# Attention stage of a graph network: two score banks and four turning banks instead of three and three, weighing two steps behind instead of three, a new order of VectorE's steps

## The reference, cut to what matters

```python
q = ((x @ Wq[l].T + bq[l]) * scaling).reshape(n, H, DH)
k = (x @ Wk[l].T).reshape(n, H, DH)
v = (x @ Wv[l].T).reshape(n, H, DH)
scores = jnp.einsum('ehd,ehd->eh', q[tgt], k[srcidx])
m = jax.ops.segment_max(scores, tgt, num_segments=n)
p = jnp.exp(scores - m[tgt])
s = jax.ops.segment_sum(p, tgt, num_segments=n)
w = p / (s[tgt] + 1e-16)
agg = jax.ops.segment_sum(w[:, :, None] * v[srcidx], tgt, num_segments=n)
attn = agg.reshape(n, D) @ Wo[l].T + bo[l]
x = _batchnorm(x + attn, g1[l], beta1[l])
ff = jax.nn.relu(x @ W1[l].T + b1[l]) @ W2[l].T + b2[l]
x = _batchnorm(x + ff, g2[l], beta2[l])
```

## Time and profile before

| | |
|---|---|
| median of the runs | 3730.28 us (3718.55 to 3731.51, 3 runs) |
| the profiled execution | 3731.51 us |
| its span, first to last instruction | 3729.7 us |
| mean granted TensorE clock | 0.932 of full speed |
| TensorE busy with matmuls | 3060.9 us, 82% |
| VectorE busy | 2398.0 us, 64% |
| GpSimd busy | 2258.4 us, 61% |
| ScalarE busy | 1894.0 us, 51% |
| first and last score matmul | 1198.9 us and 3536.5 us |

### The profile page before, as it was taken

One profiled execution on the slowest core, in us unless ns is written; L12 is line 12 of the kernel. 1 busy time (PEld: TensorE's weight loads), 2 busy tenths in 40 slices (PEclk: granted clock), 3 DMA queues, 4 the chain that ended last, 5 costly groups with the idle time before them and its releaser, 6 DMA issues. The chain is left out here.

```text
span 3729.7 us, 71602 instructions
## 1 busy us (share of the span) xinstructions
PE 3060.9 (82%) x24162; PEld 2383.1 (64%) x24162; DVE 2398.0 (64%) x6716; ACT 1894.0 (51%) x3792; POOL 2258.4 (61%) x1979
## 2 busy tenths in 40 slices
PE   1461995465798999999999988997999999999982
PEld 1220442232475787888888877775887788888871
DVE  7898452232212777888888865116887788888858
ACT  0120342122222777777777751225777777777712
POOL 2888888888000777767777750005776777777703
PEclk9995997777899999999999988998999999999995
DMA  9444643433314999999999960218998999999804
GB/s 365 59 83 91 139 106 55 89 69 55 107 45 89 152 165 159 161 159 160 161 164 166 165 113 34 54 45 153 163 164 160 162 158 165 160 163 164 151 19 115
DMA packets 1332714, 476.46 MB, mean 128 GB/s; under 512 B 1286534, under 2 KB 1312159, under 8 KB 1323558
## 3 DMA queue, kind: packets, MB, share of 16 engines
q1 hardware_dynamic: 1191472, 440.24, 61.2%
q0 software_dynamic: 133120, 0.80, 3.6%
q10 hardware_dynamic: 7788, 31.21, 2.5%
HBM read 138.70 MB, written 70.75 MB: 56 GB/s over the span
## 5 line engine op out<-in xcount | busy, mean ns | idle before, releaser
L1174 DVE CUSTOM_DVE_ANT_0 prob<-s_ps,mask 125x500 f32<-125x500 f32 x1600 | 1063.3, 673 | 334.2 <-PE s_ps L1021 245.2
L952 POOL TENSOR_TENSOR staged<-prob,staged 125x500 f16<-125x500 f32 x960 | 1065.6, 1116 | 169.8 <-ACT staged L946 108.3
L1111 ACT ACTIVATE prob<-prob,neg_max 125x1000 f32<-125x1000 f32 (+1 forms) x960 | 954.1, 994 | 151.3 <-DVE scrap L1180 150.3
L1021 PE MATMUL s_ps<-keys,queries 128*125 128x500 f16 x3200 | 946.7, 378 | 26.0 <-DMA queries<-q_feat 19.5
L372 POOL DMA_INDIRECT counts<-count,cell x320 | 758.9, 2371 | 167.4 <-issue 95.0
L1052 PEld LDWEIGHTS o_ps<-values,across 125*125 125x125 f16 x7680 | 591.1, 139 | 227.1 <-issue 78.5
L1052 PE MATMUL o_ps<-values,across 125*125 125x128 f16 x7680 | 608.5, 222 | 60.0 <-DMA across<-staged 59.1
L946 POOL CAST staged<-prob 125x500 f16<-125x500 f32 x640 | 385.6, 603 | 418.9 <-ACT prob L1111 277.2
L1187 DVE TENSOR_TENSOR p_lo<-t_ps,p_hi 125x500 f16<-125x500 f32 x640 | 431.8, 675 | 74.5 <-ACT p_hi L1121 73.6
L1121 ACT CAST p_hi<-t_ps 125x500 f16<-125x500 f32 x640 | 359.5, 562 | 113.6 <-PE t_ps L1032 113.3
L1032 PE MATMUL t_ps<-identity,prob 125*125 125x125 f32 x2560 | 406.5, 281 | 0.1
(11 more groups left out here) (139 smaller groups left out, 3731.4 us busy)
## 6 DMA issues: line engine op xcount, KB each, us to landing
mask<-bias_rows SPq DMA_DIRECT2D x200, 218.8 KB
counts<-xt ACTq DMA_DIRECT2D x8, 3054.0 KB, 38.2
parts<-counts SPq DMA_DIRECT2D x20, 1093.8 KB
bias_rows<-edge_bias SPq DMA_DIRECT2D x20, 1093.8 KB
queries<-q_feat SPq DMA_DIRECT2D x160, 125.0 KB, 3.8
pair_row<-pair_flat SPq DMA_DIRECT2D x40, 437.5 KB
across<-staged SPq DMA_TRANSPOSE x960, 3.3
counts<-count,cell POOLq DMA_INDIRECT x320, 4.2
```

The lines of the kernel that those rows point to most:

```text
L952: engine.tensor_tensor(here[0:P, BPC:2 * BPC, 0:P], prob[u % PROBS][:, k * KC:(k + 1) * KC].rearrange("p (s c) -> p s c", s=BPC), here[0:P ...
L1021: mm = pe.matmul(s_ps[n % SB][:, 0:KC], lhsT=queries[b][:, h, part, :], rhs=keys[:, h, c * KC:(c + 1) * KC], start=(part == 0), stop=(part ...
L1111: act.activation(here, here, ACT.Exp, bias=neg_max[u % 4][:, :], accum_out=sums[u // H % 2][:, u % H, piece:piece + 1]).then_inc(exped, 1)
L1174: dve.tensor_tensor_reduce(out=prob[u % PROBS][:, at], in0=s_ps[n % SB][:, 0:KC], in1=bias[b][:, at], scale=1.0, scalar=MASKED, op0=ALU.ad ...
```

## The change

Five things change. The score banks become two and the turning banks four. TensorE weighs two chunks behind instead of three; with LAG, ScalarE's read_high moves to k = 2 and VectorE's read_low to k = 3. In VectorE's program low_half(u, k) and read_low(u - 1) now stand ahead of add_bias(u + 2, k). The steps T and O stand at k = 1 and k = 3 of h = 1, 2 and 3, two in each, and bn_stats one head earlier. TensorE's wait for `wo_sb` moves from the first O step to ahead of the layer's first score.

```diff
-SB = 3
-TB = 3
-HEAD0 = 5
+SB = 2
+TB = 4
+HEAD0 = 4
...
-LAG = 3
+LAG = 2
...
-EXTRA = {(1, 2): ("T", 0), (2, 0): ("T", 1), (2, 2): ("O", 0), (3, 0): ("O", 1), (3, 2): ("O", 2), (4, 0): ("O", 3)}
+EXTRA = {(1, 1): ("T", 0), (1, 3): ("T", 1), (2, 1): ("O", 0), (2, 3): ("O", 1), (3, 1): ("O", 2), (3, 3): ("O", 3)}
...
                 def times_wo(t, o):
                     n, r = use("O", t, o)
                     user_done(pe, n - TB)
-                    if t == 0:
-                        pe.wait_ge(wo_loaded, 16 * (layer + 1))
                     pe.wait_ge(agg_turned, 2 * (T0 + t) + 2)
...
+                pe.wait_ge(wo_loaded, 16 * (layer + 1))
                 for u in range(2):
                     for c in range(NKC):
                         score(u, c)
...
                 for u in range(UNITS):
                     for k in range(NKC):
+                        if k in BY_PE:
+                            low_half(u, k)
+                        if k == LAG + 1 and u > 0:
+                            read_low(u - 1)
                         if u + 2 < UNITS:
                             add_bias(u + 2, k)
-                        if k in BY_PE:
-                            low_half(u, k)
-                        if k == min(LAG + 1, NKC - 1) and u > 0:
-                            read_low(u - 1)
                         stage_lows(u, k + NKC)
```

## The result

The changed kernel takes 3830.73 us (median of 4 runs, 3824.95 to 3835.14), the kernel before 3728.45 us beside it: a ratio of 1.0279, with an interval from 1.0254 to 1.0303. It is slower by about 102 us; the forecast was 3810, with a range to 3859. The profiled execution's span is 3822.8 us, 93 us over the one before. There attention of layer 0 began some 9.5 us earlier than in the execution before (SyncE's first load of queries at 1182.72 in place of 1192.26 us), which is the stage ahead of it, untouched by the change; so some 102 us belong to attention here too.

The account below looks back on a forecast made before the run. TensorE, busy 914.77 of 960 us, was taken as the bound before. A tile of 51.6 us, 1.4 over 50.14, gave 55 us over 38 tiles; with 22.6 for wo, 3731.5 + 78 = 3810, range 3762 to 3859.

Parts of the forecast that it names:

- the wait for wo: At each layer's first score: TensorE waits for SyncE's last load, 11.4 + 11.2 = 22.6 us, uncovered.
- The circle through two banks: In plain units: a closed chain through TensorE, ScalarE, VectorE and two score banks takes 5.87 us, against TensorE's own 5.41.
- The second circle: VectorE's chain through maximum, exponentials, halves and adds: 5.6 to 5.75 us, longer than 5.41 but shorter than 5.87.
- The other units: Head 1: 6.87 us, as normalising delays VectorE; heads 2 and 3: 7.33 each, with two O; head 0: 5.87.
- the transposes: Weighs stand one step nearer to their DMA transposes: 0.4 us a tile taken, bounds nothing and 1.3.
- bn_stats: On VectorE after maximum of h = 3: delays score 2 of h = 4 in every second tile, 0.3 us.
- What was removed: At the first O step: TensorE's wait for ScalarE's copy of T, all 0.8 us a tile counted as gone.
- the first rival: The rival "TensorE stays the bound": tile at its floor of 47.6 us, 3657 us in all; chance 0.07.
- TensorE stays the bound: Rival: circle shorter than 5.41 us, waits gone, tile 47.6 us, 3657 in all; decides from 0.46 us; chance 0.07.
- the circle bites only in part: Rival: the circle costs 0.1 us a plain unit, not 0.46, and the tile takes some 49.6; chance 0.05.
- The transposes bind: Rival: with the shorter lag, weighs wait 2.0 us a tile in place of 0.4, 3871 us; chance 0.08.
- The clock falls: Rival: TensorE's pauses put 3.4 us of every tile at the lower clock level, 3875 us; chance 0.04.

Follow-up runs that it names:

- a1: Changed kernel with TensorE's wait for wo back at the first O step of tile 0: 3812.02 us, ratio 1.0231 to the kernel before.
- b4: Kernel before with two score banks and four turning banks alone: 3740.36 us, ratio 1.0026.
- b5: Kernel before with VectorE's new order alone (low half and read_low ahead of the add): 3743.02 us, ratio 1.0025.
- b7: Kernel before with two score banks, four turning banks and VectorE's new order together: 3801.38 us, ratio 1.0199.
- a2: Changed kernel with three score banks and three turning banks again: 3782.47 us, ratio 1.0147 to the kernel before.
- a3: Changed kernel with VectorE's old order again (add_bias ahead of low_half and read_low): 3797.16 us, ratio 1.0180 to the kernel before.
- b3: Kernel before with a lag of two alone: 3764.32 us, ratio 1.0079.
- b2: Kernel before with the new places of T and O, and bn_stats one head earlier, alone: 3728.95 us, ratio 0.9987.
- b1: Kernel before with TensorE's wait for wo ahead of the layer's first score alone: 3756.73 us, ratio 1.0081.
- a4: Changed kernel with a lag of three again: 3795.41 us, ratio 1.0184 to the kernel before.

## Why the prediction was right, and where its sizes were off

The direction, the wait for wo and the circle came out; the time is 21 us over the forecast. That lies in the tile, 51.6 us forecast, 52.4 and 52.2 measured: 83 us over the 38 tiles where 55 were forecast.

**The wait for wo**: 22.6 us forecast, 22.3 read from the two traces; 19 by a1. The agreement is partly luck: in layer 1 the load landed after 7.0 us and not 8.0, and in layer 0 the first add came 1.30 us behind the first score (1204.70 to 1206.00) and not 0.8. The granted clock was 0.50 from 1204 to 1210 us, where the forecast took a score's duration at 1.00; no run separates what that cost.

**The circle through two banks**: 5.87 us forecast, 5.91 to 6.05 measured in units without extra work (h = 4 without bn_stats, 5, 6, 7). Its legs came out as read before the change, but for 0.01 to 0.03 us at four of them (1.40 for 1.37, 0.61 for 0.58, 0.60 for 0.59, 0.73 for 0.74). Over four plain units of a tile that is some 0.4 us. b4, b5 and b7 show the cause: both edits are needed, and with either undone (a2, a3) the first plain units of a tile are back at 5.42.

**The second circle** was rightly sized (5.73 by a2) but wrongly described as one that would set TensorE's pace if the first were gone. It sets the pace only after several units, in h = 7 (5.73 us in a2 and b5).

**The other units**, on average over both layers without the first and last tile: h = 1 6.87 us forecast, 7.24 measured; h = 2 and 3 7.33 each forecast, 7.39 and 7.30 measured; h = 0 5.87 forecast, 6.24 measured. Half of the h = 1 units wait for no transpose, and they take 6.74, somewhat less than forecast, as the product in normalising came out shorter than the earlier trace rows had it (last section); the h = 0 units without such a wait take 6.00. So the transposes are the term that was too small: 0.4 us a tile was taken, while they lengthen h = 1 by some 0.5 and h = 0 by 0.24, together 0.7, as 12.9 / 18 = 0.7 us in the table of waits says too. The plain units and the transposes are the missing 0.7 us a tile; bn_stats cost 0.33 a tile, 0.3 forecast.

**What was removed**: no wait of O for the copy is left, as forecast. But it is not shown that the new places did it: with the places of before this wait is also nearly gone in b3 (1.2 us) and b7 (0.7), and with the new places alone, in b2, 8.8 us of 15.3 remain. And b2 shows that this gain, 0.8 us a tile in the prediction, cannot be had alone in the kernel before. The 3657 us of the first rival took all waits as gone; none of the twelve kernels got below a tile of 50.1 in layer 0.

**The rivals.** "TensorE stays the bound" failed at its own condition, 0.46 us of the circle, and so did "the circle bites only in part": a plain unit lost 0.5 us and more, not 0.1. "The transposes bind" was right as to the mechanism where units are short (a3: 32.4 us of waits, b3: 53.6), and wrong for the changed kernel, where they wait 12.9 us.

**How the parts add up.** By their ratios the five alone cost 30 (b1), -5 (b2), 29 (b3), 10 (b4) and 9 us (b5), 73 in all, each with an interval of some 7 to 12 us to either side, so the sum with some 20; the whole costs 104. Three comparisons show where they don't add. The pair b4 and b5 costs 74 in place of 19: 55 more, the circle. The new places of T and O, worth nothing alone, are worth some 30 us beside the pair: a4 is b7 with them and the early wait for wo, and is at 3795, while b7 with 20 to 30 us for wo would be at 3820 to 3830; its tile is 51.3 and b7's 52.3. (The 30 us is a difference of three measured ones, uncertain by some 18.) In b7 three of the four O steps stand on the circle of h = 3 and 4 (7.61 and 6.72 us, 0.8 over b4's); in a4 two stand at k = 3, behind the turn of chunk 3, and units of h = 3 take TensorE's own 7.30. The lag costs 35 us beside all this (a4 against the changed kernel) and 29 alone, but not by the same way: alone it is waits for transposes, less what O's wait for the copy gives back; in the changed kernel a part of it is read_low, which moves from behind low_half's next add into the circle and takes its unit from 5.8 to 5.95 us. 73 + 55 - 30 + 6 = 104; this comes out by construction, since each term is a difference of the same measured times, and the 6 is well inside the intervals. A check from outside is a3, which lacks the circle: it is where the other four alone put it, 30 - 5 + 29 + 10 = 64 over the kernel before, measured 1.8%, 67. So my expectation of 3700 for a3 failed on sizes: the lag costs 1.1 us a tile, the banks alone 0.4, and the new places bring nothing where I had counted 0.8 to 0.9.

"The clock falls" did not occur: from 1240 to 2200 us the granted clock is 1.00 in the changed kernel too, though TensorE pauses in nearly every plain unit. Only one stretch of some 3.4 us, from 2060.3, stood at 0.50, and the kernel before had one as long, from 1260.7.

```profile
core 0: us, PE busy (x) PEld busy (x) DVE busy (x) ACT busy (x) POOL busy (x), PEclk, DMA share, GB/s
1240.00:2200.00 960.00, 918.37 (x9153) 770.16 (x9152) 745.87 (x2378) 721.32 (x1504) 656.43 (x735) 1.00 0.90 155
```

The Trainium skill (TensorE: Matmul & The Clock Gate, A second HAM failure mode: psum-queue depth-cycling) tells of a kernel in which short pauses made the clock swing between its levels; the measurement shows no such swinging here. The row is also a warning: TensorE's busy time is 918 us here and was 915, although it did 4% less work (9153 matmuls in place of 9539). Short pauses vanish between matmuls whose ends are modelled, so the distance between equal instructions shows what the busy share doesn't.

## What to carry to other kernels

Write down, for each engine's program, the closed chain that one unit needs through the buffers, from start to start, and compare it with the busiest engine's own period; one bank fewer and other work moved ahead of the read that frees it may each cost little and together close such a chain. A chain longer than the period but with room to spare is paid late, after the lead is used up. And a place that is worth nothing alone may be worth much beside another edit: undo one part at a time and also do one alone, and read who waits in each.

## What the runs showed of the hardware that I had not expected

The normalising product (L1205 or L1206, 125 x 512 elements, VectorE) takes 0.69 us or about 1.31 us, and which of them goes with what GpSimd does at that moment. In the kernel before its median is 1.312 us, in the changed kernel 0.692 (above), in b3, which has only the lag of two, 0.691; it is about 0.69 in all five kernels with a lag of two. One execution of each kind, VectorE first, then the GpSimd instructions around it; before:

```profile
1672.90 1.28 DVE L1206 TENSOR_TENSOR agg<-agg,inverse 125x512 f32<-125x512 f32 x1
```

```profile
1672.53 2.62 POOL L952 TENSOR_TENSOR staged<-prob,staged 125x500 f16<-125x500 f32 x2
```

and after:

```profile
1690.59 0.69 DVE L1205 TENSOR_TENSOR agg<-agg,inverse 125x512 f32<-125x512 f32 x1
```

```profile
1688.12 2.17 POOL L952 TENSOR_TENSOR staged<-prob,staged 125x500 f16<-125x500 f32 x2
1691.90 0.60 POOL L946 CAST staged<-prob 125x500 f16<-125x500 f32 x1 [1.61 <-ACT prob L1110]
```

Before, GpSimd works through the whole product; after, it is idle from 1690.29 to 1691.90. Over all 40 in each kernel: before, 35 were slow, with GpSimd busy during 85% of their time on average; after, 39 were fast, with GpSimd idle throughout. Over all 560 executions in the fourteen profiles, 279 took over 1 us, and in each of these GpSimd worked at its differences (L952) for more than half of the time; 281 took up to 0.8 us, and in 269 of them it did no such work at all. Twelve of the short ones did overlap with it, so the overlap alone does not decide. GpSimd's differences stretch too: in the kernel before the 56 that overlap a product take 1.27 us on average and up to 1.57, all others at most 1.12. That the two engines share something is what I take from it; it was not tested by itself.
